# Two-layer decoder on one core: the opening stage and layer 0's self attention become one program per engine

## What is computed

```
x = x + L0_attn (norm(x))        # 32 heads of 16, q and k layer-normed, linear bias per head, causal
x = x + L0_xattn(norm(x), ctx)   # 32 query heads of 128, 8 key heads
x = x + L0_ffn  (norm(x))        # base matrix and 8 low-rank experts
x = x + L1_attn (norm(x))        # 32 heads of 16, 8 key heads
x = x + L1_xattn(norm(x), ctx)
x = x + L1_ffn  (norm(x))        # sign matrix
```

```
qkv = clip(h @ Wqkv.T, -8, 8); q, k, v = split(qkv)
q = layer_norm(q, q_ln_w, q_ln_b); k = layer_norm(k, k_ln_w, k_ln_b)
probs = softmax(q @ k.T / 4 + slope * (key - query), causal)
x = x + (probs @ v) @ Wout.T
```

## Time and profile before

| | us |
|---|---|
| median of 3 runs (lowest, highest) | 1085.3 (1083.7, 1087.15) |
| the profiled execution, device time | 1088.79 |
| its span | 1087.0 |
| DVE busy over the span | 840.0 (77%) |
| PE busy over the span | 924.5 (85%) |
| POOL busy over the span | 688.1 (63%) |
| ACT busy over the span | 635.3 (58%) |

### The profile page before, as it was taken

One profiled execution on the slowest core, in us unless ns is written; L12 is line 12 of the kernel. 1 busy time (PEld: TensorE's weight loads), 2 busy tenths in 40 slices (PEclk: granted clock), 3 DMA queues, 4 the chain that ended last, 5 costly groups with the idle time before them and its releaser, 6 DMA issues. The chain is left out here.

```text
span 1087.0 us, 21724 instructions
## 1 busy us (share of the span) xinstructions
PE 924.5 (85%) x6402; PEld 471.0 (43%) x6504; DVE 840.0 (77%) x2078; ACT 635.3 (58%) x1762; POOL 688.1 (63%) x670
## 2 busy tenths in 40 slices
PE   2389998679977799999999999998679978898567
PEld 1134454334432355555555555554234435555243
DVE  6579999438882899999999999998585746676485
ACT  3368788623432666666666766666342248888451
POOL 2659898626664677766666666674474345665393
PEclk9989999779999999999999999999889988998779
DMA  9269999934435465555655555655341258887555
GB/s 351 88 110 165 155 171 170 165 95 123 80 64 127 94 128 130 117 124 117 132 118 117 120 117 124 130 120 117 107 97 30 49 136 130 135 151 139 136 93 141
DMA packets 384003, 136.20 MB, mean 125 GB/s; under 512 B 369728, under 2 KB 370368, under 8 KB 381504
## 3 DMA queue, kind: packets, MB, share of 16 engines
q1 hardware_dynamic: 383936, 135.39, 60.3%
HBM read 42.01 MB, written 2.10 MB: 41 GB/s over the span
## 5 line engine op out<-in xcount | busy, mean ns | idle before, releaser
L157 PE MATMUL bank<-w_hi,hT 128*128 128x512 f16 (+2 forms) x1024 | 322.9, 371 | 32.9 <-PEq L350 12.5
L157 PE MATMUL bank<-w_lo,hT 128*128 128x512 bf16 (+2 forms) x469 | 171.9, 369 | 0.0
L157 PE MATMUL bank<-w_hi,small 128*128 128x512 f16 x512 | 162.8, 379 | 9.3 <-DVE small L1470 8.3
L157 PEld LDWEIGHTS bank<-w_hi,hT 128*128 128x128 f16 (+1 forms) x1024 | 100.4, 99 | 138.6 <-issue 31.9
L842 ACT ACTIVATE big<-bank,small 128x128 f32<-128x128 f32 x512 | 145.0, 385 | 21.5 <-DVE small L931 21.0
L1304 POOL TENSOR_TENSOR small<-small,mhalf 128x4 f32<-128x4 f32 x64 | 64.5, 1008 | 127.9 <-DVE small L975 127.9
L710 POOL TENSOR_TENSOR big<-big 128x512 f16<-128x512 f32 x96 | 116.7, 1222 | 34.3 <-DVE big L940 19.9
L931 DVE TENSOR_REDUCE small<-bank 128x4 f32<-128x512 f32 x128 | 86.7, 686 | 48.1 <-PE bank L758 46.9
L157 PE MATMUL bank<-small,big 128*128 128x17 f16 (+2 forms) x1728 | 106.7, 195 | 11.0 <-DMA big<-big 7.4
L1401 ACT ACTIVATE small<-small 128x128 f32<-128x128 f32 x256 | 98.8, 389 | 0.0
L157 PEld LDWEIGHTS bank<-small,big 128*128 128x128 f16 (+1 forms) x1728 | 70.7, 98 | 59.7 <-issue 15.3
(11 more groups left out here) (196 smaller groups left out, 2019.5 us busy)
## 6 DMA issues: line engine op xcount, KB each, us to landing
stage<-in_weights SPq DMA_DIRECT2D x16, 1024.0 KB, 5.3
stage<-in_weights SPq DMA_DIRECT2D x64, 256.0 KB, 2.9
big<-big SPq DMA_TRANSPOSE x168, 3.3
x<-in_x SPq DMA_DIRECT2D x2, 1024.0 KB, 6.1
big<-in_ctxT SPq DMA_DIRECT2D x1, 2048.0 KB, 16.6
big<-in_ctx SPq DMA_DIRECT2D x2, 1024.0 KB, 7.0
out<-x SPq DMA_DIRECT2D x8, 256.0 KB, 2.3
big<-in_vectors SPq DMA_DIRECT2D x5, 256.0 KB, 11.6
```

The lines of the kernel that those rows point to most:

```text
L157: last = nc.tensor.matmul(out, lhs(a, c), rhs(b, c), start=start and n == 0, stop=stop and n == 3 * chunks - 1)
```

## The change

`begin_layer` is gone. Its steps go into a new class `Opening`, whose methods are called from the program of the first attention, one list of steps per engine (`FILL_ORDER`), in which the opening's steps and those of the attention's fill stand in one order. The loop and the drain keep `SELF_ORDER`. No work is dropped. What differs in the work itself:

- the weight matrices q, k, v and out are split in four chunks of 512 columns each: ACT makes hi chunk by chunk, DVE makes lo of chunks 0 and 2, POOL of chunks 1 and 3; each product of batch 0 waits for its chunk only;
- `x` is loaded in three pieces (batches 0 and 1, 2 and 3, 4 to 7), the context in two, into `small` and not `big`, and the order of loads is another;
- statistics, root and scaling are done for each batch by itself;
- tables and vectors are prepared by steps `prep` in the lists, and the first steps that need them wait for them;
- PE turns batches in banks 4 and 5;
- there is no meeting of all engines between opening and attention;
- `weight_hi` runs two batches ahead and not three, `weight_lo` none and not one.

`EarlyRows` and its hook are removed too.

```diff
+FILL_ORDER = {
+    "tensor": """
+        row_turn_0_0 row_turn_0_1 q_0_0 q_1_0 q_2_0 q_3_0 k_0_0 k_1_0 k_2_0 k_3_0 q_0_1 row_turn_0_2 q_1_1 q_2_1 v_0_0
...
+class Opening:
...
+    def subtract_matrix(self, eng, i, c):
+        full, hi, lo = self.pieces(i, c)
+        return eng.tensor_tensor(lo, full, hi, ALU.subtract)
...
+            if i >= 2:
+                self.wait_matrix(sp, i - 2, CH - 2)
+                self.wait_matrix(sp, i - 2, CH - 1)
+            chip.load_weight(sp, W_QKVO + i, i % 2)
...
+        if what == "row_stats":
+            st, mv = chip.st[:, 6 * b:6 * b + 6], chip.mv[:, 2 * b:2 * b + 2]
+            dve.wait_ge(self.x_in[min(b // 2, 2)], 16)
+            nc.vector.bn_stats(st, chip.x[:, b * D:(b + 1) * D]).then_inc(self.measured, 1)
+            dve.wait_ge(self.measured, 2 * b + 1)
+            nc.vector.bn_aggr(mv, st).then_inc(self.measured, 1)
+            dve.wait_ge(self.measured, 2 * b + 2)
+            nc.vector.tensor_scalar(chip.ve[:, b:b + 1], mv[:, 1:2], EPS, None, ALU.add).then_inc(self.var, 1)
...
-        for it in range(-far, 1):
-            plain(it)
+        if opening is None:
+            for it in range(-far, 1):
+                plain(it)
+        else:
+            own = {"sync": opening.sync, "gpsimd": opening.gpsimd, "tensor": opening.tensor, "scalar": opening.scalar,
+                   "vector": opening.vector}[name]
+            for what, n, b in opening.order[name]:
+                own(eng, what, n, b)
+                step(what, n, b)
...
+                if batch0(b):
+                    opening.wait_matrix(pe, ("q", "k", "v").index(what), n)
...
-        begin_layer(chip, [(W_QKVO + i, i) for i in range(4)], [W_XK, W_XK + 1], start=True)
-        run(chip, lambda sem: [self_attention(chip, sem, 0, {"q": 0, "k": 1, "v": 2, "o": 3}, 4, [W_XV, W_XV + 1])])
+        run(chip, lambda sem: first_layer(chip, sem))
```

More of the change, by code:

```diff
@@ L191, in spread @@
     return ap.unsqueeze(2).to_broadcast([P, n, m])
[L194 to L270, removed]
@@ L524, in self_attention @@
+def self_attention(chip, sem, layer, slots, coming, prefetch, opening=None):
     nc, io = chip.nc, chip.io
@@ L582, in self_attention @@
                      scaled=k_scaled, normed=k_normed, hi=k_hi, lo=k_lo, turned=k_turned)}
-    setups = 7 if first else 4
-    staged = list(chip.n_staged)
+    setups = 4
+    batch0 = lambda b: first and isinstance(b, int) and b == 0
+    staged = list(chip.n_staged) if opening is None else [s + 16 for s in opening.staged]
     background = Splitting(chip, sem, coming, staged, NB, None if first else 1)
@@ L727, in step @@
                 bank = A[1] if what == "v" else A[0]
+                if batch0(b):
+                    opening.wait_matrix(pe, ("q", "k", "v").index(what), n)
+                if first and n == 0 and what == "q" and isinstance(b, int):
+                    opening.wait_rows(pe, b)
                 if n == 0:
@@ L812, in step @@
                     act.wait_ge(r["normed"], b + 1)
+                    if batch0(b):
+                        act.wait_ge(prepared_pool, 2 if what == "q_hi" else 3)
                 after(act, r["turned"][n], b * 16)
@@ L866, in vector, with prepare @@
     def vector(dve):
[L867 to L874 removed]
+        def prepare(n):
+            if n == 0:
+                nc.vector.memset(v_hi, 1.0).then_inc(prepared, 1)
+            if n == 1:
+                nc.vector.memset(v_lo, 0.0).then_inc(prepared, 1)
+            if n == 2:
+                dve.wait_ge(opening.ident_in, 16)
+                nc.vector.tensor_copy(ident, chip.ident[:]).then_inc(prepared, 1)
+            if n == 3:
+                dve.wait_ge(opening.tables_in, 32)
+                nc.vector.tensor_copy(heads(causal), chip.big[:, CAUSAL].unsqueeze(1).to_broadcast([P, GH, P])
+                                      ).then_inc(prepared, 1)
+        if not first:
+            for n in range(2):
+                prepare(n)
             for t in (qs, ks):
                 nc.vector.memset(t, 0.0).then_inc(prepared, 1)
[L877 removed]
+            dve.wait_ge(prepared, setups)
         def step(what, n, b):
+            if what == "prep":
+                prepare(b)
             if what in ("q_clip", "k_clip"):
@@ L1994, with last_stages @@
 }
[L1997 removed]
+def last_stages(chip, sem, sign_slot, seen):
     nc, io = chip.nc, chip.io
@@ L2015, in last_stages @@
     S, T, Y, A = ([chip.psum[i] for i in pair] for pair in ((0, 2), (3, 4), (5, 1), (6, 7)))
-    first = early.rows
+    first = TurnedRows(chip, sem, "first", first_scratch)
     second = TurnedRows(chip, sem, "second", second_scratch)
```

358 lines of the change are left out of this document (180 added, 178 removed).

## The result

The changed kernel takes 1067.78 us in the median of 4 runs (1067.03 to 1071.52), beside 1086.22 us for the kernel before in the same series (4 runs, 1083.7 to 1092.17). The ratio is 0.9827, 95% interval 0.9802 to 0.9853: 18.8 us faster, between 16.0 and 21.5. The forecast was 15.8 us and a time of 1069.5.

What follows compares the result with a forecast made beforehand. A chain bounds the opening and the fill's start, then DVE is nearly full. The first addition ends at 89.5 instead of 105.3 us, saving 15.8: 1085.3 - 15.8 = 1069.5 us, range 1061 to 1079.

Steps and rivals of the forecast that it cites:

- The chain comes forward by 31 to 32 us: Opening and start of fill: first transpose at 23.5 against 54.40 us, first scores near 30 against 62.16.
- Most of it is not kept, since the deferred work fills DVE: Up to the first addition: DVE's 78.8 us of work puts its end at 89.5, not 105.3, saving 15.8 us.
- The queue has 13 us of slack under DVE, as a mean: DMA queue in the fill: 29 transposes and three 1 MB loads end at 76 us, 13 us of slack under DVE.
- The second rival: Loads between the fill's transposes stall the pipe; one event costs 6.3 us, giving 1075.8 us; chance 0.22.
- DVE as the one bound: Fill up to the first addition: DVE's work sets the length; POOL, ACT, PE and the queue end no later.
- density: DVE's busy share in the fill from 30 us: 89% gives an end at 90 us, the loop's 96% gives 86.
- The third rival: PE's clock stays at its lower level in the fill, 12 us a batch; two batches give 1093 us; chance 0.05.
- below 0.9: Sign of the PE clock loss: granted PE clock under this value from 30 us to the loop.
- The port pair: DVE and POOL share SBUF ports as an exclusive lock, so overlap lengthens both; nothing added, price already in the rows.
- A loss or gain behind the first addition: Loop and after: order unchanged, additions of batches 0 to 4 still 18.7 to 20 us apart; no cause for loss.

Runs made afterwards that it cites:

- e12: The changed kernel with 1 MB more loaded near 65 us, ahead of the second matrix of the next stage; ratio to the kernel before 0.9832, first addition 4.2 us later.
- e11: The changed kernel with the splitting of the context on ACT and POOL moved from the fill into the drain; ratio to the kernel before 0.9814.
- e2: The changed kernel with each of the eight context copies on ACT made twice, 4.4 us more ACT work; ratio to the kernel before 0.9836.

## Why the prediction was right

- **The chain comes forward by 31 to 32 us: right.** 32.0 at the first product, 28.2 at the first transpose (26.16, forecast 23.5), 30.7 at the first scores. The terms of 2.46 us for each MB held up to matrix k; the vectors let POOL start at 17.80 and not 16.3, and matrix v came at 21.17 and not 19.5. And two steps were mis-sized by the same oversight, that DVE's list stands in order: two chunks of k took 3.20 us beside POOL, and `q_norm` stands behind a statistics step and k's clip, so it began at 22.34, not 18.9.
- **Most of it is not kept, since the deferred work fills DVE: right, and the sum was good.** Start 5.51 (forecast 5.2), busy 77.00 (78.8), end 87.62 (89.5). The added instructions came as worked out (chunks 8.2 us for 8.1). The 1.9 us that were missed are the busy time, 1.8 too high (the scaling took 7.4 and not 8.1, and the casts of the preparing steps 0.6 less; the rest is not assigned). A fit this close is partly luck: the same DVE work reads 74.4 to 77.0 us in other kernels of this study.
- **"The queue has 13 us of slack under DVE, as a mean": this step failed.** The mean was right (share 0.84 over the whole stretch) and of no use. The slack lay before 50 us (share 0.62 from 31.4 to 50); behind it the share is 0.92 to 1.01, and e12 pays for its load in full. The second rival, which put a price on loads between transposes, named this mechanism, with 6.3 us an event; 2.35 is what e12's load put on the queue. The changed kernel's own load at 64.43 stands right behind the place of e12's extra one and may cost as much; no run takes it away. The time came out all the same.
- **DVE as the one bound: only partly.** 4.9 us more on it cost 2.7, 3.9 us less gave 1.4, and a single bound would have passed on both nearly in full. What I called its density was the sum of several engines' orders. Behind 30 us 54.1 us of DVE's work was left, as forecast (54), but it ran at 94%, between the old fill's 89% and the loop's 96%. Why it was 94% no run shows. That the number is this good although the bound is not as told is in part luck.
- **The third rival, PE's clock: its loss did not come, its sign did.** PEclk was 0.53 from 26.2 to 31.4 and 0.90 up to the first addition (0.97 before). From 30 us to the first addition it was 0.88, and "below 0.9" there was the sign. The loop ran at 1.00 from the first turn on. The price is open. As an estimate from these figures, 0.10 of 87.62 us against 0.03 of 105.3 us is 5.6 us of PE's time, the most that it can be, if PE had never waited; a part of it may lie in the last 12.62 us, as told above.
- **The port pair.** The rule from the Trainium skill, "SBUF — State Buffer", "SBUF: two separate sides", that DVE and GpSimd exclude each other there, agrees with the 1.64 us beside POOL against 0.75 alone. How large the price is in total no run shows: the fall of DVE's busy time in e11 came in e2 too, with POOL's work unchanged. I had added nothing for it, and the rows bear that out, since the same two groups read 1283 and 1195 ns in the old fill and 1264 ns each in the new one.
- **A loss or gain behind the first addition: none was forecast, and the profiled execution gained 3.3 us** up to the last one. The table shows it to be in the spread of those turns. The median doesn't need it: 1069.5 less the 1.9 us missed at the first addition is 1067.6, and 1067.8 was measured.

## What to carry to other kernels

When two stages are merged, the time saved is not that of the chain that comes forward but what the fullest engines leave: count each engine's work up to a fixed point in both stages together, and divide by a density between that of the old fill and that of the loop. Here that came within 1.9 us, with terms that did not act quite as the sum says. Do the same for the DMA engines by halves of the stretch, not as a mean: here they were 0.62 and then 1.0, and 1 MB put nothing on the queue that lasted in the one and 2.35 us in the other. And in lists written by hand the place can be worth more than the work: seven steps moved within two lists were worth 7.2 us. Before reading differences of 1 us from single executions, look how far two kernels are apart ahead of the place where they differ.

## What I had not expected of the hardware

Busy time of DVE is elastic. With the same DVE work it reads 74.39 us in e2 and 77.00 in the changed kernel; two groups of seven instructions with operands in SBUF are at 1059 and 1085 ns in the one and at 1264 in the other, against 0.75 us alone. That they wait for POOL while counted as busy is shown for single rows (1.64 us at 23.80). An engine that reads 94% busy (DVE from 31.40 to 87.62: 53.0 of 56.2 us) may still have room.
